# A fixed slot tile per expert in a routed expert layer, with weight blocks of 64 KB in place of 96 KB

## The chip, the cores and the metric

One core of a Trainium2 chip runs the whole program. The metric is the device time of one execution in microseconds, from the first instruction to the last, with what lies around it. The kernel before takes 2897.25 us, the median of 3 runs (2891.38 to 2900.32).

## The reference, cut to what matters

Eight layers act on 4096 tokens of 128 numbers, in float32: cosine attention, routed experts, a gated recurrence (GLRU), routed experts again with the same weights, a state space layer (mamba), and three more. The change touches the two expert layers alone:

```
logits = x @ router_w.T + expert_bias          # 4096 tokens x 160 experts
probs = sigmoid(logits); top_w, top_idx = top_k(probs, 8)
top_w = 2.5 * top_w / (sum(top_w) + 1e-9)
h1 = silu(x @ w_gate[e].T)                     # 64 wide, for each expert e
out[t] = sum over the 8 experts e of t of top_w[t, e] * (h1 @ w_down[e].T) + shared expert
```

So each token meets 8 of 160 experts, and an expert is a gate matrix of 128x64 and a down matrix of 64x128. The tokens reach each layer as a layer norm of the running sum X.

## The kernel before, in words

X stays in SBUF. An expert layer (`run` 0 and 1) is worked in two halves (`h`) of 2048 tokens, 16 tiles of 128 tokens each. It has four parts.

**Routing** (`route_half`, L1634): layer norm, router product on PE, sigmoid on ACT, the eight largest on DVE, and a 0/1 MASK of 128 tokens x 160 experts for each tile.

**Slots** (`slots` L1641, `place` L1667, `rows_of_slots` L1680, on PE `count` L1873 and `rank` L1885): each assignment of a token to an expert gets a row in a DRAM table `slot_rows`. PE counts the tokens of each expert. DVE rounds the counts up to tiles of 128 rows, sums them over the experts, and so finds the first row of each expert and the expert of each tile. Then, tile after tile of tokens, `rank` adds the tokens that stand earlier to psum bank 7, `place` masks it (L1673) and takes the eight row numbers with one MAX8 (L1676), and the next `rank` waits for L1673. After each four tiles `rows_of_slots` works out the 32 row numbers per partition in six small operations (L1683 to L1691). POOL's `dispatch` (L1718) then writes each token's row with 8 indirect DMAs per tile, 128 per half.

**Expert groups** (`experts_scalar` L1767, `experts_sync` L1810, `experts_tensor` L1892, `results_out` L1693): each half has 288 slot tiles, in 72 groups of 4. Per group ACT's queue loads 256 KB of rows into XSB; PE transposes 4 tiles (L1900), ACT copies them (L1779); PE multiplies by the gate matrices (L1909), ACT takes silu (L1786), PE multiplies by the down matrices (L1918), DVE copies the results out of psum (L1699), and ACT's queue stores 256 KB to `slot_results`. SP's queue loads the weights of the 4 tiles: it reads four expert numbers into registers (L1815) and issues four DMAs of 96 KB (L1819). All buffers of a group are four deep (UNROLL), and SP may load the weights of group g only when the results of group g-4 are done (L1829). PE's order in each step is transposes of g+2, gate products of g+1, results of g. PE uses its array in parts: the gate products of two tiles stand in the two column halves (128x64 each), the result products in the two row halves (64x128 each).

**Gather** (`gather` L1728, `sum_rows` L1702): POOL fetches the 8 result rows of each token, DVE adds them weighted to X. Half 0 is gathered while half 1 is computed, half 1 while the next layer runs.

`middle_vector` and its neighbours (L1945 to L2065) write out each engine's order by hand. In run 0 both halves are routed and placed first. In run 1 half 0 is routed between steps 3 and 4 of the GLRU, its later places stand inside GLRU steps 4 to 6 (`between`), and half 1 is routed after the last GLRU step. Each engine is an in-order queue, with semaphores in between. During layer 0 SP's queue also prepares `expert_blocks` (L2098 to L2102) and zeroes `slot_rows`.

## Time and profile before

| | |
|---|---|
| runs, median (lowest, highest) | 2897.25 us (2891.38, 2900.32) |
| the profiled execution's own time | 2902.76 us |
| its span | 2900.9 us |
| mean granted TensorE clock | 0.723 |
| PE busy | 1753.3 us (60%) |
| DVE, ACT, POOL busy | 1334.2, 970.8, 1057.4 us |
| bytes moved by DMA | 393.39 MB |
| packets: under 512 B, under 2 KB, all | 57952, 222512, 332506 |
| waits of PE's gate product (L1909) for the weights | 271.0 us |

The span is that of the one core. A share of busy time is an average over stages with different limits: the four stretches of expert groups make up a third of the span, and there the DMA engines are nearly always busy. DMA issues are not counted as busy time of an engine. In the table of groups, the idle time stands beside what ended it.

### The profile page before, as it was taken

To read this page: it belongs to the slowest core of one execution; us is meant where nothing else is said; L and a number is where in the kernel's file an instruction comes from. 1 tells how busy PE (TensorE), PEld (TensorE's weight loads), DVE (VectorE), ACT (ScalarE), POOL (GpSimd) and SP (SyncE) were. 2 spreads that over 40 slices of the span, in tenths; PEclk is the share of its full clock that TensorE was granted. 3 is DMA by queue.
4 is the path that set the end of the run, shared out by engine and by line. 5 is a ranking of instruction groups with operands and counts; after the bars stand their busy time and mean duration, and the time that the engine had idled before them with its cause. 6 is when DMAs were issued, how large, how long until landed. Compare 5 with 4: busy or idle time off the path is not lost.

```text
span 2900.9 us, 44112 instructions
## 1 busy us (share of the span) xinstructions
PE 1753.3 (60%) x13716; PEld 1146.8 (40%) x13716; DVE 1334.2 (46%) x3558; ACT 970.8 (33%) x1719; POOL 1057.4 (36%) x1177
## 2 busy tenths in 40 slices
PE   3765506776666454556776676422325488888975
PEld 2544404555444242244554454100124234455443
DVE  3648811222334677473222333543215466666644
ACT  3651102232223321312232222356761123444342
POOL 2001777724651774757714651771000200000000
PEclk9985557778878655557788787655555568998985
DMA  8941118999997111117999997120000000000001
GB/s 234 382 181 29 51 53 275 325 304 292 321 289 241 52 52 54 52 55 244 327 308 294 310 301 241 51 54 8 4 2 0 0 1 1 1 1 2 1 1 29
DMA packets 332506, 393.39 MB, mean 136 GB/s; under 512 B 57952, under 2 KB 222512, under 8 KB 332208
## 3 DMA queue, kind: packets, MB, share of 16 engines
q1 hardware_dynamic: 215616, 171.43, 19.0%
q10 hardware_dynamic: 83984, 153.13, 15.4%
q0 software_dynamic: 32768, 67.17, 7.7%
q8 instruction: 65, 1.06, 0.1%
q14 instruction: 73, 0.60, 0.1%
HBM read 242.13 MB, written 164.63 MB: 140 GB/s over the span
## 4 chain that ended last, share of the span: by engine, by line
PE 36%; DVE 15%; DMA 13%; ACT 11%; issue 10%; SPq 9%; POOL 6%; DVEq 0%; ACTq 0%; POOLq 0%
DMA arena<-expert_blocks 12%; SPq L1819 6%; ACT arena L955 5%; PE psum L1918 4%; PE psum L1909 4%; POOL slot_rows L1725 4%; PE psum L448 3%; SPq L1815 3%; PE psum L1347 2%; PE psum L1900 2%; PE psum L1328 2%; PE psum L432 2%; PE psum L993 1%; PE psum L427 1%; ACT arena L1210 1%
## 5 line engine op out<-in xcount | busy, mean ns | idle before, releaser
L1736 POOL DMA_INDIRECT arena<-slot_results,SLOTS x512 | 490.7, 958 | 503.1 <-DMA slot_results<-arena 285.8
L1725 POOL DMA_INDIRECT slot_rows<-arena,SLOTS x512 | 493.4, 964 | 309.4 <-issue 308.8
L1699 DVE COPY arena<-psum 128x512 f32<-128x512 f32 x288 | 198.6, 690 | 742.3 <-PE psum L1918 719.4
L1909 PE MATMUL psum<-arena 128*64 128x128 f32 x2304 | 236.5, 336 | 278.4 <-DMA arena<-expert_blocks 271.0
L1779 ACT ACTIVATE arena<-psum 128x512 f32<-128x512 f32 x288 | 171.9, 597 | 476.4 <-PE psum L1900 467.6
L1909 PEld LDWEIGHTS psum<-arena 128*64 128x64 f32 x2304 | 154.5, 165 | 349.0 <-issue 291.5
L169 POOL TENSOR_SCALAR rstd<-mv 128x4 f32<-128x4 f32 x32 | 6.2, 193 | 772.3 <-DVE mv L577 771.8
L1900 PE MATMUL psum<-ident,arena 128*128 128x128 f32 x1152 | 231.6, 335 | 84.9 <-DMA arena<-slot_rows 84.3
L1918 PE MATMUL psum<-arena 64*128 64x128 f32 x2304 | 253.3, 350 | 0.0
L1786 ACT ACTIVATE arena<-psum 128x256 f32<-128x256 f32 x288 | 110.4, 383 | 338.5 <-PE psum L1909 335.3
L1918 PEld LDWEIGHTS psum<-arena 64*128 64x128 f32 x2304 | 189.6, 230 | 64.4 <-issue 64.2
L1900 PEld LDWEIGHTS psum<-ident,arena 128*128 128x128 f32 x1152 | 149.6, 166 | 130.0 <-issue 93.4
L1710 DVE SCALAR_TENSOR_TENSOR X<-arena,WEIGHTS,X 128x128 f32<-128x128 f32 x512 | 180.2, 352 | 39.9 <-DMA arena<-slot_results,SLOTS 23.9
L955 ACT ACTIVATE arena<-arena 128x1 f32<-128x1 f32 x510 | 150.0, 294 | 16.5
L602 PE MATMUL psum<-ident,XN 128*128 128x128 f32 x192 | 44.4, 376 | 169.4 <-DVE XN L590 165.1
L1101 DVE TENSOR_REDUCE arena<-psum 128x1 f32<-128x128 f32 x256 | 74.0, 289 | 101.4 <-PE psum L1347 96.6
L1210 ACT ACTIVATE arena<-psum 128x1536 f32<-128x1536 f32 x64 | 92.8, 1449 | 80.5 <-PE psum L432 80.5
L602 PEld LDWEIGHTS psum<-ident,XN 128*128 128x128 f32 x192 | 33.2, 197 | 199.7 <-issue 188.2
L1102 DVE TENSOR_REDUCE arena<-psum 128x1 f32<-128x256 f32 x256 | 105.8, 413 | 0.0
L448 PE MATMUL psum<-arena 128*32 128x256 f32 (+1 forms) x1536 | 95.9, 357 | 8.6 <-ACT arena L1210 5.4
L448 PE MATMUL psum<-arena,ones 128*32 128x256 f32 (+1 forms) x1536 | 89.1, 336 | 0.0
L427 PE MATMUL psum<-arena 51*128 51x256 bf16 (+1 forms) x384 | 64.4, 283 | 40.1 <-ACT arena L349 22.5
(234 smaller groups left out, 3064.5 us busy)
## 6 DMA issues: line engine op xcount, KB each, us to landing
arena<-expert_blocks SPq DMA_DIRECT2D x1152, 96.0 KB
arena<-slot_rows ACTq DMA_DIRECT2D x288, 256.0 KB
slot_results<-arena ACTq DMA_DIRECT2D x288, 256.0 KB
slot_rows<-zeros SPq DMA_DIRECT2D x2, 18432.0 KB, 84.2
slot_rows<-arena,SLOTS POOLq DMA_INDIRECT x512, 2.2
arena<-slot_results,SLOTS POOLq DMA_INDIRECT x512
expert_blocks<-in_expert_w SPq DMA_DIRECT2D x1, 7680.0 KB, 26.0
expert_blocks<-in_expert_w SPq DMA_DIRECT2D x1, 5120.0 KB, 52.7
```

Of the source, the lines that this page charges most:

```text
L448: mm = pe.matmul(psum[32 * r:32 * r + 32, 3, 256 * half + lo:256 * half + hi], ones4[:, head_of(n, r) % 4, :] if half else vp(kt, head_of( ...
L955: act.activation(H[:, g, t:t + 1], U[:, g, t:t + 1], ACT.Tanh, bias=H[:, g, t - 1:t]).then_inc(m_h[g], 1)
L1210: act.activation(PR2[:, g % 2], psum[:, 4:8, 0:384], ACT.Exp, scale=DH ** -0.5).then_inc(r_exp.sem, 1)
L1699: dve.tensor_copy(YSB[:, p].rearrange("p (c h) d -> p h c d", h=2), psum[:, first:first + 2, 0:256].rearrange("p h (c d) -> p h c d", c=2) ...
L1710: dve.scalar_tensor_tensor(X[:, t, :], GATHERED[:, j, k], WEIGHTS[:, t, k:k + 1], X[:, t, :], ALU.mult, ALU.add).then_inc(g_sum.sem, 1)
L1725: pool.indirect_dma_start(out=slot_rows[h], out_offset=bass.IndirectOffsetOnAxis(ap=SLOTS[:, t, k:k + 1], axis=0), in_=XNH[:, t], in_offse ...
L1736: pool.indirect_dma_start(out=GATHERED[:, t % TPI, k], out_offset=None, in_=slot_results[h], in_offset=bass.IndirectOffsetOnAxis(ap=SLOTS[ ...
L1779: act.activation(XSBT[:, g % UNROLL], psum[:, g % 2, :], ACT.Copy).then_inc(c_xt.sem, 1)
L1819: sp.dma_start(EWB[:, p, q], expert_blocks[bass.ds(e * P, P), :]).then_inc(c_ew[p].sem, 16)
L1900: mm = pe.transpose(psum[:, p % 2, P * q:P * q + P], XSB[:, p, q], ident[:])
L1909: mm = pe.matmul(psum[lo:lo + INTER, 2 + 5 * (p % 2), o:o + P], EWB[:, p, q, 0:INTER], XSBT[:, p, P * q:P * q + P], start=True, stop=True, ...
L1918: mm = pe.matmul(psum[:, 3 + 2 * (p % 2) + q % 2, c:c + P], HEB[lo:lo + INTER, p % 2, c:c + P], EWB[lo:lo + INTER, p, q, INTER:EW], start= ...
```

## The change: what it does

Each expert now owns one slot tile of 128 rows whatever its count (160 own tiles, 40 groups). An expert with more than 128 tokens in the half takes its further rows from 128 overflow tiles (32 groups), which are handed out as before by counts. There are still 72 groups of 4 tiles; GROUP_ORDER mixes the two kinds evenly.

Because own tiles have known experts, their weights are loaded with fixed addresses: four DMAs, each of 32 partitions with 2 KB in a row. Overflow groups still read four expert numbers and issue four DMAs of 128 pieces of 512 B. For that `expert_blocks` is laid out by partition, and a block is 128x128 (64 KB): 64 columns of gate, 64 of down. The down matrix is cut in column halves, of which one stands in partitions 0 to 63, the other in 64 to 127. So that each result half finds its silu in its own partitions, the gate matrix must stand twice side by side: DVE writes that copy (`gates_twice`), the gate product gives 128 output rows instead of 64, silu covers 512 columns instead of 256, and the results are 8 products of 64x128 by 64x64 per group instead of 4 of 64x128 by 64x128.

Slot numbers need more work: after each four tiles DVE compares, shifts the rows beyond the own tile, scans over 640 elements, masks, takes MAX8, and subtracts neighbours.

```diff
-        EW = INTER + D
+        EW = INTER + D // 2
...
+        GROUP_ORDER = sorted(range(GROUPS), key=lambda n: (n + 0.5) / OWN_GROUPS if n < OWN_GROUPS else (n - OWN_GROUPS + 0.5) / MORE_GROUPS)
...
+        def own_tiles(dve):
+
+            dve.tensor_tensor_scan(OWN_END, ones_row[:], ones_row[:], 0.0, ALU.mult, ALU.add).then_inc(o_own, 1)
...
+            dve.tensor_scalar(OWN_END, OWN_END, float(P), None, ALU.mult).then_inc(o_own, 1)
...
+            dve.tensor_scalar(OWN, OWN_END, -float(P), None, ALU.add).then_inc(o_own, 1)
...
         def slots(dve, run, h):
...
+            dve.tensor_scalar(NTILES, NTILES, 0.0, None, ALU.max).then_inc(link.sem, link.one())
...
+            dve.tensor_tensor(DELTA, DELTA, OWN_END, ALU.subtract).then_inc(link.sem, link.one())
...
         def place(dve, run, t):
...
-            dve.max(S8[:, j], SLOTM[:, j]).then_inc(s_s8.sem, 1)
...
         def rows_of_slots(dve, run, i):
...
-            dve.tensor_scalar(SLOT[:], S8[:], -1.0, None, ALU.add).then_inc(s_slot.sem, 1)
...
+            dve.tensor_tensor(OVER, SLOTM, every(OWN_END), ALU.is_gt).then_inc(link.sem, link.one())
+            dve.wait_ge(link.sem, link.so_far())
+            dve.tensor_tensor(OVER, OVER, every(DELTA), ALU.mult).then_inc(link.sem, link.one())
+            dve.wait_ge(link.sem, link.so_far())
+            dve.tensor_tensor(OVER, SLOTM, OVER, ALU.add).then_inc(link.sem, link.one())
...
+            dve.tensor_tensor_scan(PLACED.rearrange("p t e -> p (t e)"), ones_row[:, 0:1].broadcast_to([P, TPI * NE]), OVER.rearrange("p t e -> p (t e)"),
+                                   0.0, ALU.mult, ALU.add).then_inc(link.sem, link.one())
...
+            dve.tensor_tensor(PLACED, PLACED, MASK[:, TPI * i:TPI * i + TPI, :], ALU.mult).then_inc(link.sem, link.one())
...
+            for j in range(TPI):
+                last = TOPK * (TPI - 1 - j)
+                dve.max(S8[:, last:last + TOPK], PLACED[:, j]).then_inc(link.sem, link.one())
...
+            dve.scalar_tensor_tensor(SLOT[:].rearrange("p t k -> p (t k)"), S8[:, 0:TPI * TOPK], -1.0, S8[:, 1:TPI * TOPK + 1],
+                                     ALU.add, ALU.subtract).then_inc(link.sem, link.one())
...
+        def gates_twice(dve, run, h, g):
+
+            p, hr = g % UNROLL, HALVES * run + h
+            dve.wait_ge(c_ew[p].sem, c_ew[p].at(hr, g // UNROLL))
+            dve.tensor_copy(GATES[:, p], EWB[:, p, :, 0:INTER].unsqueeze(2).broadcast_to([P, GROUP, 2, INTER])).then_inc(c_twice.sem, 1)
...
             def gated(g):
-                act.activation(HEB[:, g % 2], psum[:, 2 + 5 * (g % 2), 0:256], ACT.Silu).then_inc(c_he.sem, 1)
+                act.activation(HEB[:, g % 2], psum[:, 2 + 5 * (g % 2), :], ACT.Silu).then_inc(c_he.sem, 1)
...
         def experts_sync(sp, run, h):
...
+            def own_weights(n, p):
+                for part in range(GROUP):
+                    rows = slice(P // GROUP * part, P // GROUP * (part + 1))
+                    sp.dma_start(EWB[rows, p].rearrange("p q c -> p (q c)"), expert_blocks[rows, GROUP * EW * n:GROUP * EW * (n + 1)]).then_inc(c_ew[p].sem, 16)
...
-                    sp.dma_start(EWB[:, p, q], expert_blocks[bass.ds(e * P, P), :]).then_inc(c_ew[p].sem, 16)
+                    sp.dma_start(EWB[:, p, q], expert_blocks[:, bass.ds(e * EW, EW)]).then_inc(c_ew[p].sem, 16)
...
             def inner(g, p):
-                pe.wait_ge(c_ew[p].sem, c_ew[p].at(hr, g))
+                pe.wait_ge(c_twice.sem, c_twice.at(hr, g, p + 1))
...
-                    mm = pe.matmul(psum[lo:lo + INTER, 2 + 5 * (p % 2), o:o + P], EWB[:, p, q, 0:INTER], XSBT[:, p, P * q:P * q + P],
-                                   start=True, stop=True, skip_group_check=True, tile_position=(0, lo))
+                    mm = pe.matmul(psum[:, 2 + 5 * (p % 2), P * q:P * q + P], GATES[:, p, q].rearrange("p a c -> p (a c)"),
+                                   XSBT[:, p, P * q:P * q + P], start=True, stop=True, skip_group_check=True)
...
             def results(g, p):
...
-                    mm = pe.matmul(psum[:, 3 + 2 * (p % 2) + q % 2, c:c + P], HEB[lo:lo + INTER, p % 2, c:c + P],
-                                   EWB[lo:lo + INTER, p, q, INTER:EW], start=True, stop=True, skip_group_check=True, tile_position=(lo, 0))
+                    for half in range(2):
+                        lo = INTER * half
+                        mm = pe.matmul(psum[:, 3 + 2 * (p % 2) + half, INTER * q:INTER * q + D // 2], HEB[lo:lo + INTER, p % 2, P * q:P * q + P],
+                                       EWB[lo:lo + INTER, p, q, INTER:], start=True, stop=True, skip_group_check=True, tile_position=(lo, 0))
...
         def middle_vector(dve):
...
                 for g in range(GROUPS):
+                    if g + 2 < GROUPS:
+                        gates_twice(dve, run, 0, g + 2)
                     results_out(dve, run, 0, g)
...
-            whole = a["expert_w"].rearrange("(e p) c -> e p c", p=P)
-            block_of = expert_blocks.rearrange("(e p) c -> e p c", p=P)
+            whole = a["expert_w"].rearrange("(e p) c -> p e c", p=P)
+            block_of = expert_blocks.rearrange("p (e c) -> p e c", c=EW)
```

## Rows read from the trace of the kernel before

**Rows 1.** Stretches: us; PE, PEld, DVE, ACT, POOL busy; PEclk, DMA share, GB/s.

```profile
447.00:684.00 237.00, 170.81 (x1440) 125.26 (x1440) 49.67 (x72) 71.56 (x145) 119.70 (x125) 0.80 0.95 309
684.00:933.00 249.00, 167.94 (x1440) 123.04 (x1440) 93.98 (x208) 72.04 (x146) 121.16 (x128) 0.80 0.93 297
...
sum 970.00, PE 673.61 PEld 493.66 DVE 287.02 ACT 285.95 POOL 475.47; mean PE 168.40 PEld 123.41 DVE 71.76 ACT 71.49 POOL 118.87
```

**Rows 2.** DMA queues (packets, MB, share), 447 to 684: ACT's, SP's, POOL's.

```profile
q10 hardware_dynamic: 20457, 37.26, 46.2%
q1 hardware_dynamic: 40307, 27.53, 39.2%
q0 software_dynamic: 4064, 8.33, 9.2%
```

**Rows 3.** Chain of waits, 611 to 625 us: start, duration, what.

```profile
611.50 0.02 SPq L161
...
614.02 4.92 DMA arena<-expert_blocks
...
624.74 0.02 SPq L161
```

**Rows 4.** Timeline of PE, expert groups: start, duration, line, shapes.

```profile
619.16 1.12 PE L1909 MATMUL psum<-arena 128*64 128x128 f32 x8 [2.78 <-DMA arena<-expert_blocks]
...
622.41 1.12 PE L1909 MATMUL psum<-arena 128*64 128x128 f32 x8
...
625.55 0.66 PE L1909 MATMUL psum<-arena 128*64 128x128 f32 x8
626.14 0.72 PE L1918 MATMUL psum<-arena 64*128 64x128 f32 x8
626.79 0.66 PE L1900 MATMUL psum<-ident,arena 128*128 128x128 f32 x4
627.37 0.66 PE L1909 MATMUL psum<-arena 128*64 128x128 f32 x8
```

**Rows 5.** Timeline of PE elsewhere, eight fp32 passes on the whole array.

```profile
1092.74 1.13 PE L1856 MATMUL psum<-w_sh_gate,arena 128*128 128x64 f32 x8
2847.43 1.16 PE L822 MATMUL psum<-w_wv_t,arena 128*128 128x128 f32 x8 [0.66 <-DVE arena L752]
```

**Rows 6.** Timeline, last place of the first four tiles, and what follows.

```profile
277.57 0.32 DVE L1673 SCALAR_TENSOR_TENSOR arena<-psum,arena 128x160 f32<-128x160 f32 x1
279.54 0.32 DVE L1673 SCALAR_TENSOR_TENSOR arena<-psum,arena 128x160 f32<-128x160 f32 x1
280.46 1.22 POOL L1725 DMA_INDIRECT slot_rows<-arena,SLOTS  x1 [106.01 <-issue]
```

**Rows 7.** Groups by line: busy us, mean ns of one, idle before.

```profile
L1620 DVE TENSOR_TENSOR arena<-arena 128x640 f32<-128x640 f32 x16 | 13.2, 825 | 0.5
L1618 DVE TENSOR_TENSOR_SCAN arena<-ones_row,arena 128x160 f32<-128x160 f32 x64 | 26.3, 473 | 2.3
L653 DVE TENSOR_TENSOR_SCAN arena<-arena 128x256 f32<-128x256 f32 x16 | 10.2, 678 | 1.4 <-DVE arena L647 1.4
L1624 DVE MAX8 C<-arena 128x8 f32<-128x160 f32 x64 | 16.2, 315 | 2.4
```

**Rows 8.** Timeline of DVE, a place inside the GLRU and DVE's next work.

```profile
1145.11 0.33 DVE L1673 SCALAR_TENSOR_TENSOR arena<-psum,arena 128x160 f32<-128x160 f32 x1
1148.82 0.69 DVE L661 TENSOR_TENSOR arena<-psum,arena 128x512 f32<-128x512 f32 x1 [1.84 <-ACT arena L689]
```

**Rows 9.** Timeline, the last place of run 1 and PE's first gate product.

```profile
1318.89 0.33 DVE L1673 SCALAR_TENSOR_TENSOR arena<-psum,arena 128x160 f32<-128x160 f32 x1
1321.30 1.12 PE L1909 MATMUL psum<-arena 128*64 128x128 f32 x8
```

**Rows 10.** Two further stretches in the columns of Rows 1.

```profile
180.00:200.00 20.00, 17.58 (x295) 11.49 (x296) 5.44 (x9) 10.74 (x10) 0.00 (x0) 0.96 0.01 3
380.00:447.00 67.00, 0.00 (x0) 0.00 (x0) 0.00 (x0) 0.00 (x0) 50.75 (x53) 0.50 0.16 56
```

More of the change, by code:

```diff
@@ L1646, in slots @@
             dve.wait_ge(link.sem, link.so_far())
-            dve.tensor_scalar(COUNT, COUNT, P - 1, None, ALU.add).then_inc(link.sem, link.one())
+            dve.tensor_scalar(COUNT, COUNT, -1, None, ALU.add).then_inc(link.sem, link.one())
             dve.wait_ge(link.sem, link.so_far())
@@ L1673, in place @@
             dve.scalar_tensor_tensor(SLOTM[:, j], psum[:, 7, 0:NE], 1.0, MASK[:, t, :], ALU.add, ALU.mult).then_inc(s_slotm.sem, 1)
-            dve.wait_ge(s_slotm.sem, s_slotm.at(run, t))
-            stand(dve)
-            dve.max(S8[:, j], SLOTM[:, j]).then_inc(s_s8.sem, 1)
             if j == TPI - 1:
@@ L1687, in rows_of_slots @@
[L1687 to L1691 removed]
+            link = Order(s_slot, run, i)
@@ new lines, in rows_of_slots @@
+            every = lambda row: row.unsqueeze(1).broadcast_to([P, TPI, NE])
+            dve.wait_ge(s_slotm.sem, s_slotm.at(run, TPI * i + TPI - 1))
+            dve.tensor_tensor(OVER, SLOTM, every(OWN_END), ALU.is_gt).then_inc(link.sem, link.one())
+            dve.wait_ge(link.sem, link.so_far())
+            dve.tensor_tensor(OVER, OVER, every(DELTA), ALU.mult).then_inc(link.sem, link.one())
+            dve.wait_ge(link.sem, link.so_far())
+            dve.tensor_tensor(OVER, SLOTM, OVER, ALU.add).then_inc(link.sem, link.one())
@@ L1878, in count @@
             mm.then_inc(e_cnt.sem, 1)
-            pe.wait_ge(o_link.sem, o_link.at(run, h))
-            pe.matmul(psum[:, 7, 0:NE], ident[:], FIRST, start=True, stop=True, skip_group_check=True)
+            pe.wait_ge(o_own, 3)
+            pe.matmul(psum[:, 7, 0:NE], ident[:], OWN, start=True, stop=True, skip_group_check=True)
+            pe.wait_ge(o_col.sem, o_col.at(run, h))
             for q in range(GROUP):
@@ L1947, in middle_vector @@
             dve.memset(C9[:], 0.0)
+            dve.memset(S8[:], 0.0)
+            own_tiles(dve)
             for h in range(HALVES):
@@ L1953, in middle_vector @@
             for run in range(HALVES):
+                for g in range(2):
+                    gates_twice(dve, run, 0, g)
                 for g in range(GROUPS):
+                    if g + 2 < GROUPS:
+                        gates_twice(dve, run, 0, g + 2)
                     results_out(dve, run, 0, g)
+                for g in range(2):
+                    gates_twice(dve, run, 1, g)
                 for g in range(GROUPS):
+                    if g + 2 < GROUPS:
+                        gates_twice(dve, run, 1, g + 2)
                     results_out(dve, run, 1, g)
@@ L2097, in _ @@
             sp.wait_ge(loaded, 16 * (FIRST_WEIGHTS + 1))
-            whole = a["expert_w"].rearrange("(e p) c -> e p c", p=P)
-            block_of = expert_blocks.rearrange("(e p) c -> e p c", p=P)
-            sp.dma_start(block_of[:, 0:INTER], whole[:, 0:INTER]).then_inc(blocked, 16)
-            sp.dma_start(block_of[:, INTER:, 0:INTER], whole[:, INTER:, 0:INTER]).then_inc(blocked, 16)
-            sp.dma_start(block_of[:, INTER:, INTER:], whole[:, 0:INTER, INTER:]).then_inc(blocked, 16)
+            whole = a["expert_w"].rearrange("(e p) c -> p e c", p=P)
+            block_of = expert_blocks.rearrange("p (e c) -> p e c", c=EW)
+            sp.dma_start(block_of[:, :, 0:INTER], whole[:, :, 0:INTER]).then_inc(blocked, 16)
+            for half in range(2):
+                sp.dma_start(block_of[INTER * half:INTER * half + INTER, :, INTER:], whole[0:INTER, :, INTER + D // 2 * half:INTER + D // 2 * (half + 1)]).then_inc(blocked, 16)
             sp.wait_ge(constants, 14)
```

97 lines of the change are left out of this document (57 added, 40 removed).

## The prediction

> **What bounds the kernel now.** I read the stretches first. Four of them hold the expert groups, 72 groups each: half 0 takes 237 us, half 1 takes 249 us, and with their like in run 1 they make 970 us [rows 1]. That is 3.29 and 3.46 us per group. In them the DMA engines show a share of 0.95 and 0.93, PE is busy for 171 of 237 us at a granted clock of 0.80, and DVE, ACT and POOL have much room [rows 1]. Next the queues: in half 0, ACT's queue (rows in, results out) takes 46.2% of the engines' time, SP's (weights) 39.2%, POOL's (scatter) 9.2% [rows 2]. Last the chain of waits, for what a full DMA does to the order of work: it goes round a ring of four groups. SP is released at 611.50, its fourth issue is out at 614.02, the weights land 4.92 us later, PE works 5.6 us, and SP is released again at 624.74 [rows 3]. That is 13.24 us for four groups, or 3.31 per group, which is the stretch's pace. So weights bound these stretches, by bytes and by latency at once; PE idles about 66 us per half.
>
> Ahead of the groups lie chains that the change lengthens: DVE's slot numbers, which release POOL's dispatch in run 0, and DVE and PE in turn in run 1.
>
> **DMA work of a group.** A weight packet now costs 0.392 x 16 x 237 us / 36,864 = 40 ns (768 B; the 3,443 others are small and counted in). ACT's 18,432 packets of 2 KB cost 95 ns each by the same division [rows 2]. A line through both gives 7.5 ns + 0.0427 ns per byte, so 29 ns for 512 B, an estimate from these rows. The 40 own groups need 128 packets of 2 KB, the 32 overflow groups 512 of 512 B: (5,120 x 95 + 16,384 x 29) / 16 = 60 us of all engines per half, against 93 now. With ACT's 109.5 and POOL's 21.8 unchanged, half 0 needs 192 us of DMA instead of 224. At today's 0.95 that is 202 us; half 1, by the same saving, 215. If bytes count and not packets (73.2 MB less 9.4), the bounds are 206 and 217. Above that the only bound is no gain at all, 237, should 512 B pieces at a wide pitch cost the 40 ns of 768 B and more.
>
> **PE work of a group.** At the full clock today: gate products 0.59 us (625.55 to 626.14), results 0.65, transposes 0.58, together 1.82 us; at the half clock the same three take 3.25 us (619.16 to 622.41) [rows 4]. After:
> - Gate products: 8 passes on the whole array in place of 8 on halves. Such passes take (1.16 - 0.27) / 7 = 0.127 us each at the full clock, with 0.27 us the last one's tail [rows 5]. 8 x 0.127 = 1.02 us.
> - Results: 16 passes with 64 moving columns in place of 8 with 128. No row shows that form packed in row halves. Below: the moving columns are the same in number, so 0.65 us. Above: the unpacked form with 64 columns costs (1.13 - 0.27) / 7 = 0.122 us [rows 5], 16 x 0.122 = 1.95 us. I take 0.078 us per pass. Two packed passes today cost 2 x 0.081 = 0.162 us, 0.035 more than one unpacked pass of the same width (0.127); I put the same 0.035 on the unpacked narrow pass, (0.122 + 0.035) / 2. That gives 1.25 us.
> - Transposes stay at 0.58.
>
> Sum 2.85 us, or 205 us per half at the full clock (2.25 to 3.55 us, 162 to 256 us, by the two bounds). At the half clock, in proportion, 3.25 x 2.85 / 1.82 = 5.1 us. So PE, today with a third of its time idle, comes level with DMA.
>
> The first row on this is that 8 result passes with 128-column weights take 0.65 us, 81 ns each, at the full clock [rows 4]. The Trainium skill (TensorE: Matmul & The Clock Gate, "LDWEIGHTS (loading the stationary operand)") says that a weight load costs its columns divided by 1.2, whatever the rows: 107 ns here. By that rule 16 result passes could not be under 1.71 us, the group would be 3.3 us and half 0 would gain nothing. The 81 ns contradict the rule as a floor for packed loads, so the sum stays with the rows.
>
> **The ring after.** From one release of SP to the next, at the full clock: issue 2.1 us (2.5 today [rows 3]; the register load goes in 40 of 72 groups), flight 3.9 us (4.92 today; a quarter of the packets in the own groups, bounds 2.5 and 5.5), DVE's copy of the gates 0.8 with a wait behind L1699 (640 elements take 0.825 [rows 7], 512 so 0.66), PE 1.02 + 1.25 + 2.85 = 5.1. Sum 11.9 us, 2.98 per group. Three limits so stand close together (DMA 2.8, PE 2.85, ring 2.98), and where one is late the others can't make it up. I add 2% for that and take 3.05 in half 0 if the clock were full, and 3.1 in half 1, where the DMA has 8 us more to do. The clock: PE falls to half speed after waits such as the 2.78 us before 619.16 and is back by 625.55 [rows 4]. With PE over 90% busy such waits must be rare; I take 3% of the groups at 5.1. The result is 3.11 and 3.16 us per group, 224 and 228 us. Against 237 and 249, twice, the stretches give back 2 x (13 + 21) = 68 us.
>
> The rest of the edit inside the groups is hidden. Silu over 512 columns: ACT is busy 72 of 237 us [rows 1] and works a step ahead of PE. The gate copies add 72 x 0.66 = 48 us to DVE's 94 in half 1 [rows 1]; DVE copies two groups ahead, so the 3 us of a gather sum in front of one copy fits in two groups of PE work. If that cover failed, each of 16 sums per half would cost up to 3 us, 96 us in all.
>
> **Slot numbers.** For four tiles, the last place and the first of the next four lie 1.97 us apart, with 0.32 for L1673 itself [rows 6]. Of the work in between, 0.4 us (one MAX8) goes, and there come: compare, multiply, add and mask, four operations over 640 elements, 4 x 0.87 with the step between them [rows 7]; one scan over 640, (0.678 - 0.473) / 96 per element, 1.5 us (up to 4 x 0.473 = 1.9) [rows 7]; four MAX8 in a row, 4 x 0.25 = 1.0 (0.315 each, overlapped [rows 7]); a small subtraction for a small one. In all 3.5 + 1.5 + 1.0 + 0.2 - 0.4 = 5.8 us more. Where this is late:
> - Run 0, half 0, first four tiles: POOL starts at 280.46 [rows 6] and issues on, one DMA in 1.26 us, until the groups start (53 in the last 67 us, with every other engine idle [rows 10]), so all of it counts: 5.8. `own_tiles` adds 1.3 at the start of routing, `slots` 0.3 for one operation on 160 elements, and the first rank matrix no longer waits for DVE, -0.9. Sum 6.5. The other seven blocks of run 0 delay only DVE's routing, which is done 67 us ahead of POOL [rows 10]: 7 x 5.8 = 41 us fit in, nothing.
> - Run 1, half 0, first four: the GLRU's front stands behind it in DVE's queue: 5.8 - 0.6 = 5.2.
> - Three blocks inside the GLRU: after the place at 1145.11 DVE's next work starts at 1148.82 [rows 8]. The chain now ends at 1145.44 + 7.4 = 1152.8, so 4.0 us each, 12.0.
> - Run 1, half 1: nothing stands between the places and the groups. Three blocks of 5.8, less 0.6: 16.8. The fourth holds back the first gate copy: today the first gate product starts 2.1 us after the last place ends [rows 9], then 7.4 + 0.7 = 8.1 us after, so 6.0.
>
> Sum 6.5 + 5.2 + 12.0 + 22.8 = 46.5 us. Bounds 35 (small operations overlap more) and 60.
>
> **The preparation of the blocks** becomes 40,960 pieces of 256 B. DMA is idle from 180 us on [rows 10] and the first scatter is at 280 us, so up to 100 us more are hidden; past that each microsecond delays POOL.
>
> **Sum.** 2902.8 (the profiled execution) - 68 + 46.5 = 2881; that execution is 5.5 us above the median, so 2876 us.
>
> **Rivals.**
> A. PE becomes the bound and slower than today's pace. Place: the results products; price: 0.107 to 0.122 us per pass instead of 0.078, 3.3 to 3.55 us per group. It decides from 0.107 on: half 0 no longer gains. For it: the form is unknown, and the narrow unpacked pass is hardly cheaper than the wide one [rows 5]. Against: halves do overlap today. At 0.122, 256 us in each of four stretches, +54 and +46: 2997; at 0.107, 240 each, -10 and +46: 2933.
> B. The clock stays at 0.80 as today, 40% of the groups' time at the half clock: 0.6/3.05 + 0.4/5.1 = 0.275 groups per us, 3.63 us, 262 us per stretch: 3016. For it: PE's waits for weights are what drops the clock, and some will remain. Against: a PE that is always due has no waits of 2.8 us.
> C. The narrow passes cost near their floor (0.06 us) and DMA alone sets the pace: 202 and 215 us, -136 and +46: 2807. For it: packing hid half the time so far. Against: the ring needs 2.9.
> D. The change doesn't do what it says: 512 B pieces cost as much as 768 B, and the ring stays at 3.2 to 3.3: -25 and +46: 2918.
>
> **How the numbers follow.** Forecast 0.40 (its own range 2850 to 2906), C 0.18, D 0.16, A 0.17, B 0.09. A measurement here tells about 0.3%, 8.7 us, from no change: faster is below 2888.6, same up to 2905.9. The forecast's mass is three quarters faster, the rest nearly all the same; C is faster; D is a quarter same, the rest slower; A and B slower. Faster 0.48, same 0.14, slower 0.38. The range leaves out the lower end of C and A's upper half with B: 2810 to 2965.
>
> **What would show it.** Right: weight packets fall to 60 us of engine time per half; L1900's group period near 3.1; PE busy over 90% of a stretch at a clock over 0.9; results pass 0.078 at the full clock; POOL's first scatter about 6.5 us later; the stretch from GLRU's fourth step to the groups about 40 us longer. Wrong: PE idle as before, a clock near 0.8, or result passes over 0.1.

## The result, and the profile after

The changed kernel takes 2968.61 us, the median of 4 runs (2959.92 to 2976.76), against 2894.32 us for the kernel before in its 4 runs beside it (2889.72 to 2900.32). The ratio is 1.0255, 95% interval [1.0219, 1.0291]: 74 us slower. I had forecast 2876 us. The profiled execution after took 2959.92 us with a span of 2958.0 us, 57.1 us more than the span before.

Where the 57.1 us stand, from the first and last work of the expert groups in the two traces:

| stretch | before | after | change | forecast |
|---|---|---|---|---|
| start to the first group of run 0 | 447.42 | 465.49 | +18.1 | +6.5 |
| the two halves of run 0 | 483.0 | 482.0 | -1.0 | -34 |
| to the first group of run 1 | 389.0 | 421.4 | +32.4 | +34.0 |
| the two halves of run 1 | 481.1 | 486.4 | +5.3 | -34 + 6.0 |
| to the end | 1100.4 | 1102.7 | +2.3 | 0 |

The 68 us that the stretches were to give back did not come at all. Of the 79 us between the forecast for the profiled execution (2881) and its time (2960), 66 lie in the stretches. The other 12 lie outside them, nearly all in the first row. Here are the four stretches of the changed kernel ("after" from here on), in the columns of [rows 1]: time; PE, PEld, DVE, ACT, POOL busy; granted clock, DMA share, GB/s.

```profile
465.00:702.00 237.00, 208.42 (x2016) 185.92 (x2016) 76.79 (x144) 87.29 (x145) 121.48 (x125) 0.90 0.85 274
702.00:948.00 246.00, 210.82 (x2016) 187.76 (x2016) 118.20 (x269) 86.00 (x144) 122.14 (x128) 0.90 0.83 258
1369.00:1607.00 238.00, 202.98 (x2016) 182.12 (x2016) 85.04 (x162) 87.28 (x145) 110.19 (x112) 0.92 0.83 266
1607.00:1855.00 248.00, 215.72 (x2014) 193.75 (x2016) 119.06 (x268) 85.89 (x144) 122.58 (x128) 0.87 0.83 255
sum 969.00, PE 837.93 PEld 749.56 DVE 399.08 ACT 346.45 POOL 476.40; mean PE 209.48 PEld 187.39 DVE 99.77 ACT 86.61 POOL 119.10
```

The DMA engines did get their relief (share 0.95 to 0.85, rate 309 to 274 GB/s), and the clock rose (0.80 to 0.90). The time is what it was. PE is busy 208 of 237 us and the DMA share is 0.85: neither is full. The queues of half 0, as in [rows 2]:

```profile
q10 hardware_dynamic: 20687, 37.66, 46.1%
q1 hardware_dynamic: 25807, 18.75, 29.2%
q0 software_dynamic: 4064, 8.33, 9.6%
```

Weights take 0.292 x 237 = 69 us of all engines, where [rows 2] gave 93 and I had worked out 60. The chain of waits, in the part that answers to [rows 3]:

```profile
568.65 0.02 SPq L161
...
568.73 0.45 SPq L1872
...
571.28 3.81 DMA arena<-expert_blocks
...
575.12 0.44 DVE arena L1738
...
575.60 1.16 PE psum L1964 x8
576.75 1.06 PE psum L1974 x16
...
577.83 0.02 SPq L161
```

Read it from one release of SP (568.65) to the next (577.83): 2.6 us for the register load and four issues, 3.8 in flight, 0.44 for the gate copy, then the gate products of that group, and behind them, in the same step, the results of the group before. That last operation is what SP waits for. So one turn of 9.2 us covers three groups and not four: 3.06 us per group in this turn, in which nothing waits for a busy engine. Over the whole half, from the end of the fourth group's results to that of the last, the trace gives 3.16 us per group. The rest of the 237 us is the start of the stretch: 17.7 us pass from the first transposes to the end of the fourth results. In the kernel before it was 16.7 us, and then 3.19 per group. Next PE's timeline at the full clock, and one operation of each kind at the half clock (start, duration, line, shapes, wait):

```profile
577.72 0.66 PE L1956 MATMUL psum<-ident,arena 128*128 128x128 f32 x4
578.27 1.16 PE L1964 MATMUL psum<-arena 128*128 128x128 f32 x8
579.36 1.11 PE L1974 MATMUL psum<-arena 64*128 64x64 f32 x16
580.40 0.66 PE L1956 MATMUL psum<-ident,arena 128*128 128x128 f32 x4
583.94 1.15 PE L1964 MATMUL psum<-arena 128*128 128x128 f32 x8 [0.33 <-DVE arena L1738]
...
486.52 1.97 PE L1974 MATMUL psum<-arena 64*128 64x64 f32 x16
...
601.57 1.91 PE L1964 MATMUL psum<-arena 128*128 128x128 f32 x8
```

From start to start, gate products take 1.09 us (1.02 forecast), the 16 result passes 1.04 us, 0.065 each (1.25 and 0.078 forecast), transposes about 0.55. A group costs PE 2.7 us, less than my 2.85. Yet it waits again and again for L1738, the gate copy, and so in the end for weights:

```profile
L1964 PE MATMUL psum<-arena 128*128 128x128 f32 x2304 | 356.8, 304 | 119.2 <-DVE arena L1738 118.7
L1974 PE MATMUL psum<-arena 64*128 64x64 f32 x4608 | 344.8, 293 | 0.0
L1738 DVE COPY arena<-arena 128x512 f32<-128x512 f32 x288 | 126.7, 441 | 345.1 <-DMA arena<-expert_blocks 344.1
```

Those are groups of the page (busy us, mean ns, idle before). DVE's copies themselves wait 344 us for the weights. PE's wait in front of the gate products fell from 271 us to 119, while its work in the stretches grew by 164 us (673.61 in [rows 1] to 837.93): the waits were filled with work, and nothing was left over.

### The profile page after: what moved, and what is told of

Read it like the earlier page. It is cut to its first block, busy times and chain, and to the rows that moved or that the text cites. A ratio compares the mean times of both kernels' runs of the same rounds, so it can differ in the third digit from the quotient of the medians.

```text
span 2958.0 us, 46720 instructions
## 1 busy us (share of the span) xinstructions
PE 1922.6 (65%) x16020; PEld 1404.0 (47%) x16020; DVE 1517.2 (51%) x3938; ACT 1032.8 (35%) x1719; POOL 1082.8 (37%) x1177
## 4 chain that ended last, share of the span: by engine, by line
PE 40%; DVE 19%; ACT 11%; DMA 10%; issue 9%; POOL 6%; SPq 5%; DVEq 0%; ACTq 0%; POOLq 0%
DMA arena<-expert_blocks 9%; PE psum L1964 6%; PE psum L1974 6%; ACT arena L955 5%; POOL slot_rows L1776 4%; PE psum L448 3%; SPq L1876 2%; DVE X L1757 2%; PE psum L1956 2%; PE psum L1347 2%; PE psum L1328 2%; PE psum L432 2%; PE psum L993 1%; PE psum L427 1%; ACT arena L1210 1%
## 5 line engine op out<-in xcount | busy, mean ns | idle before, releaser
L1776 POOL DMA_INDIRECT slot_rows<-arena,SLOTS x512 | 515.0, 1006 | 331.8 <-issue 331.8
L1964 PE MATMUL psum<-arena 128*128 128x128 f32 x2304 | 356.8, 304 | 119.2 <-DVE arena L1738 118.7
L1964 PEld LDWEIGHTS psum<-arena 128*128 128x128 f32 x2304 | 317.3, 213 | 148.4 <-DVE arena L1738 120.4
L1974 PE MATMUL psum<-arena 64*128 64x64 f32 x4608 | 344.8, 293 | 0.0
L1830 ACT ACTIVATE arena<-psum 128x512 f32<-128x512 f32 x288 | 172.0, 597 | 488.1 <-PE psum L1956 487.1
L1974 PEld LDWEIGHTS psum<-arena 64*128 64x128 f32 x4608 | 304.1, 202 | 38.2 <-issue 8.8
L1738 DVE COPY arena<-arena 128x512 f32<-128x512 f32 x288 | 126.7, 441 | 345.1 <-DMA arena<-expert_blocks 344.1
L1837 ACT ACTIVATE arena<-psum 128x512 f32<-128x512 f32 x288 | 172.0, 597 | 277.1 <-PE psum L1964 275.6
L1956 PE MATMUL psum<-ident,arena 128*128 128x128 f32 x1152 | 205.8, 306 | 60.5 <-DMA arena<-slot_rows 60.0
L1956 PEld LDWEIGHTS psum<-ident,arena 128*128 128x128 f32 x1152 | 133.2, 151 | 82.0 <-issue 50.2
```

The costliest lines, as they stand in the source:

```text
L1738: dve.tensor_copy(GATES[:, p], EWB[:, p, :, 0:INTER].unsqueeze(2).broadcast_to([P, GROUP, 2, INTER])).then_inc(c_twice.sem, 1)
L1776: pool.indirect_dma_start(out=slot_rows[h], out_offset=bass.IndirectOffsetOnAxis(ap=slots_of(t, k), axis=0), in_=XNH[:, t], in_offset=None ...
L1830: act.activation(XSBT[:, g % UNROLL], psum[:, g % 2, :], ACT.Copy).then_inc(c_xt.sem, 1)
L1837: act.activation(HEB[:, g % 2], psum[:, 2 + 5 * (g % 2), :], ACT.Silu).then_inc(c_he.sem, 1)
L1956: mm = pe.transpose(psum[:, p % 2, P * q:P * q + P], XSB[:, p, q], ident[:])
L1964: mm = pe.matmul(psum[:, 2 + 5 * (p % 2), P * q:P * q + P], GATES[:, p, q].rearrange("p a c -> p (a c)"), XSBT[:, p, P * q:P * q + P], sta ...
```

## Experiments

The stretches of each are read from its own trace with the same cut (first transposes to last results); before gives 964 us and after 968 in that cut. A trace shows one execution, which can lie off its kernel's median, and where that matters it is said. The kernel before was run beside the others each time: it took 2901 us beside the first four, and 2889 beside the next four.

**The two parts alone.** The slots without the blocks:

```diff
-        EW = INTER + D // 2
+        EW = INTER + D
```

and with it the 96 KB blocks, packed products and 256-column silu of before.

> Fixed slot tiles, overflow tiles and the mixed order of groups, with the blocks, products and silu of the kernel before (own tiles load their 96 KB blocks from fixed addresses). Theory 1, the slot numbers: the DVE chain of 7.3 us per four tiles, and POOL held up by DVE's long operations, cost all of what lies outside the group stretches, +50 to +55 us; the stretches stay at 237 and 249 us, since their DMA work is unchanged: 2940 to 2955 us. Rival, the mixed order or the fixed loads matter: fixed loads spare SP 0.5 us per own group, which shortens the ring, 5 to 8 us per stretch less, 2915 to 2930 us.

Measured 2910.91 us, ratio 1.0042 [1.0020, 1.0064]. The blocks without the slots (EW as in the change, the doubled gates, 16 narrow result passes, every expert number read at run time):

> The 64 KB blocks, the doubled gate matrix and the narrow result products, with the slots of the kernel before, so that every group reads its experts at run time and loads 512 pieces of 512 B. Theory 1: the price of the whole change lies in the slot numbers, and what the blocks save in DMA is lost again to the longer ring (DVE's copy, longer products) and PE's half clock: stretches within 5 us of 237 and 249, in all 2885 to 2910 us. Rival, the blocks save 16 us or more per stretch by themselves (DMA work 192 in place of 224 us): 2830 to 2850 us. Second rival, PE's added work costs more than the DMA saves: 2920 us or more.

Measured 2958.79 us, ratio 1.0177 [1.0152, 1.0202]. The first stretch of each, slots alone and then blocks alone:

```profile
463.00:696.00 233.00, 164.90 (x1441) 120.93 (x1441) 49.70 (x72) 71.76 (x145) 119.61 (x126) 0.81 0.96 317
```

```profile
450.00:707.00 257.00, 220.03 (x2017) 198.04 (x2018) 77.63 (x144) 87.09 (x145) 121.58 (x126) 0.85 0.80 253
```

All four stretches take 922 us with the slots alone (-42) and 1036 with the blocks alone (+71). The profiled execution of the blocks alone was the slowest of its five, 21 us above their median, so about +50 is nearer to a usual one. So the slots save in the stretches and the blocks cost there, though the blocks are the part that takes load off DMA (0.95 to 0.80). The slots alone still lose slightly, since what they add outside the stretches, 45 us, is more than the 42. Neither is what I expected. The slots were to leave the stretches as they were, and the rival, 5 to 8 us less in each, went the right way but not far enough. The blocks did worse than my 2885 to 2910, as their second rival said. The slots come with two things, fixed expert numbers and the mixed order of groups; no run parts them.

**The rings deeper.** All rings of a group in SBUF (rows, weights, gate copies, results) six steps deep, in after and in before. For the two further steps, semaphores serve that the first layer no longer needs.

```diff
-        UNROLL = 4
+        UNROLL = 6
```

> The changed kernel with all rings of the groups six deep in place of four, nothing else. Theory 1, the ring: weights are released by the results of four groups before, but PE does the gate products of one group ahead of the results, so only three groups cover issue (2.6 us), flight (3.8 to 5), DVE's copy (0.5) and two products (2.2); with six, five groups cover them and the limit moves to DMA (share 0.85 of 237 us, so 201 us of work) or PE (2.52 us per group at the full clock, 181 us): 205 to 215 and 213 to 225 us per stretch, 2865 to 2885 us in all. Rival, DMA packets or PE's clock set the pace and depth changes nothing: 2955 to 2970 us.

Measured 2781.81 us, ratio 0.9581 [0.9558, 0.9605], 83 us below the lower end of what I expected.

> The kernel before with all rings of the groups six deep. Theory 1, there DMA is full (share 0.95 and 0.93), so depth can win only what is missing to 1: 3 to 6 us per stretch of half 0 and 8 to 12 of half 1, 2865 to 2880 us. Rival, also there the ring's latency sets the pace and the share shown is inflated by queueing: 15 us or more per stretch, under 2840 us.

Measured 2799.57 us, ratio 0.9642 [0.9621, 0.9664], where the rival had it. The first two stretches of after with six deep and, below them, the first of before with six deep:

```profile
460.00:652.00 192.00, 184.52 (x2016) 170.25 (x2016) 75.71 (x144) 87.19 (x145) 120.83 (x125) 0.98 0.99 339
652.00:857.00 205.00, 187.70 (x2016) 170.06 (x2016) 116.20 (x269) 86.02 (x144) 122.95 (x128) 0.99 0.96 307
```

```profile
448.00:667.00 219.00, 156.57 (x1440) 115.29 (x1440) 49.70 (x72) 71.72 (x145) 120.04 (x125) 0.85 1.00 334
```

This one edit is worth 171 us of stretches in after (968 to 797) and 107 in before (964 to 857). Not an instruction or a byte of a group is saved by it. PE is now busy 184.5 of 192 us, and its timeline goes round with almost no wait: PE's own passes bound this stretch now. (In the second half of each run the same kernel needs 2.79 us per group; why stays open.) Here one step, from gate products (L1972 there) over results (L1982) to the next gate products:

```profile
580.39 1.06 PE L1972 MATMUL psum<-arena 128*128 128x128 f32 x8
581.38 1.11 PE L1982 MATMUL psum<-arena 64*128 64x64 f32 x16
...
582.91 1.06 PE L1972 MATMUL psum<-arena 128*128 128x128 f32 x8
```

2.52 us per group. The clock follows: of the 144 groups of run 0, the transposes ran at the half clock in 50 in before, in 19 in after, and in 6 in after with six deep, which are the first three groups of each half (1.1 us in place of 0.66 for four tiles). With the waits gone the low clock is gone, so it was mostly a result of them. And the share of 0.95 that I had taken as DMA at its bound was none: with six deep before moved 334 GB/s where it had moved 309.

What depth bought can be read from SP. Its waits for results in the first stretch of before and, below it, of before with six deep (waited for, us, times, longest):

```profile
SPq L161 <- PE psum L1918: 184.1, 22, 166.7
```

```profile
SPq L161 <- PE psum L1926: 162.5, 1, 162.5
```

The longest wait is the one for the half's first results. Without it, SP stood waiting for 17.4 us of the stretch in before, and not at all with six deep. In after it was 58.5 us, and 5.9 with six deep. So the turn through the buffers held SP back far more in after than in before. In before SP's own stream of register loads and issues was nearly as long as the turn.

**Taking PE's and DVE's share out of the turn.** Two kernels on the changed one. In the first there is no gate copy: the gate product waits for the weights themselves and multiplies by a buffer of zeros, so the output of the experts is left out, while every operation on PE stays.

```diff
-                pe.wait_ge(c_twice.sem, c_twice.at(hr, g, p + 1))
+                pe.wait_ge(c_ew[p].sem, c_ew[p].at(hr, g))
```

> The changed kernel without the copy that doubles the gates: the gate product waits for the weights themselves and reads a GATES tile set once to zero. It leaves out the gate matrices. All products, silus and DMAs stay. Theory 1: the ring becomes 0.5 us shorter per three groups, in half 1 more, where the copy also waits behind gather sums: 0.17 us and more per group, 12 to 20 us per stretch, 2890 to 2920 us. Rival, the copy is hidden: 2955 us or more.

Measured 2932.02 us, ratio 1.0146 [1.0095, 1.0196]: less was gained than I expected, though more than the rival allows. The second also goes back to the packed products of before, on the 64 KB blocks: 8 gate passes on column halves and 8 result passes of 64 moving columns, so half of the result products is left out.

> The changed kernel with its slots, blocks and DMAs, but with the products of the kernel before: gate products of two tiles in the two column halves, 8 result passes per group over 128 columns of the block, silu over 256, no doubling copy on DVE. It leaves out the right result: the result products read gate columns as if they were the down matrix's. Theory 1, the ring of three covering groups: issue 2.6, flight 4, products 1.2 instead of 2.1 and no copy of 0.5, so 7.8 us per three groups in place of 9.2: DMA then binds, 207 to 215 us per stretch, 2840 to 2870 us. Rival, SP's issue or DMA's small pieces alone set the pace: 2940 us or more.

Measured 2852.16 us, ratio 0.9876 [0.9819, 0.9933]. First stretches, without the copy and then with the packed products:

```profile
464.00:698.00 234.00, 205.90 (x2017) 185.46 (x2018) 49.76 (x72) 87.25 (x145) 119.68 (x125) 0.91 0.87 278
```

```profile
465.00:682.00 217.00, 161.38 (x1440) 118.79 (x1439) 49.69 (x72) 71.82 (x145) 119.44 (x125) 0.83 0.93 299
```

The four stretches take 932 and 848 us, against 968 (the profiled execution is the fastest of its kernel in all three). A copy of 0.44 us on an engine that is busy 77 of 237 us costs 0.13 us per group on average. That is near the 0.15 that a turn for three groups would give (0.44 / 3), but it is no proof of the third: the first stretch gained 3 us and the others 9 to 13. And 45 us less PE work per half (205.90 to 161.38) give back 21 us per half, though PE was not full before. PE at its bound would not have answered to the copy, and DMA at its bound would have answered to neither; a turn of latencies answers to both.

**SP's issues.** The weights of an own group in one DMA of 256 KB in place of four.

```diff
-                for part in range(GROUP):
-                    rows = slice(P // GROUP * part, P // GROUP * (part + 1))
...
+                sp.dma_start(EWB[:, p].rearrange("p q c -> p (q c)"), expert_blocks[:, GROUP * EW * n:GROUP * EW * (n + 1)])
```

> The changed kernel with the weights of an own group in one DMA of 128 partitions x 2 KB instead of four of 32. Theory 1: SP issues an own group in 0.5 us instead of 1.9, so its ring is 1.4 us shorter in 40 of 72 groups, 0.25 us per group on average if all counts: up to 18 us per stretch, half of that where PE or an overflow group binds next: 2900 to 2935 us. Rival, SP's issue is hidden behind the flight of earlier pieces: 2955 us or more.

Measured 2978.22 us, ratio 1.0307 [1.0245, 1.0369], no better than the change itself; the stretches take 984 us. There are three issues fewer, but the one transfer is longer in flight than the last of four. Two such in the chain of waits:

```profile
567.02 4.42 DMA arena<-expert_blocks
...
574.27 5.98 DMA arena<-expert_blocks
```

In the mean over the first stretch it is 4.57 us, against 4.07 for the last quarter of an own group in after. From the first issue to the landing, though, the single transfer is the faster (4.57 against 5.44), and still no time was gained. The table shows where it went: the mean turn of the first stretch, in us, from the results that SP waits for to the results three groups later.

| kernel | wait for SP's queue | first to last issue | flight of the last | copy and its wait | wait for PE | gate product to results | sum |
|---|---|---|---|---|---|---|---|
| before | 1.67 | 1.59 | 4.22 | none | 0.65 | 1.64 | 9.76 |
| after | 0.56 | 1.48 | 3.89 | 0.53 | 0.72 | 2.31 | 9.49 |
| without the copy | 0.58 | 1.50 | 3.93 | none | 1.17 | 2.33 | 9.50 |
| packed products, no copy | 0.70 | 1.54 | 4.25 | none | 0.77 | 1.55 | 8.81 |
| one DMA for own weights | 0.53 | 0.71 | 4.31 | 0.81 | 1.23 | 2.34 | 9.92 |

The sum is three times the pace by its making, so it proves nothing by itself; its parts do. With one DMA the 0.77 us that the issues save came back in front of DVE and PE (0.28 and 0.51) and in the flights (0.42), which made the turn longer than in after. Why PE was later there stays open. Without the copy, too, the wait for PE took most of the 0.53 back in this stretch. So the turn is what paces after, but it has about 1.3 us of queueing in it (0.56 and 0.72), and a piece that is shortened is not always won.

**The slot numbers later.** Six deep, and in run 1 the chains of L1700 moved: those of half 0 by one GLRU step, those of half 1 between the first results of half 0.

```diff
+                    if run and g % 8 == 1 and g // 8 < HSTEPS:
+                        rows_of_slots(dve, 1, HSTEPS + g // 8)
```

> Rings six deep as in after_u6, and in run 1 the slot numbers out of the way: SLOTM holds 16 tiles, the chains of half 1 stand in DVE's queue after results 1, 9, 17 and 25 of half 0's groups, those in the GLRU at the start of the next step, where DVE is idle for 6 us. Theory 1: of the 53 us of slot numbers, 17 + 6 us before the groups of run 1 go, and 3 x 3 us in the GLRU; up to 7 us come back as stalls among the groups: 2745 to 2765 us. Rival, POOL's dispatch of half 1 starts too late or is held up by DVE's chains and the second half waits for it: 2775 us or more.

Measured 2791.58 us, ratio 0.9651 [0.9607, 0.9695], slightly worse than six deep alone. The groups of run 1 do start at 1252.3 us instead of 1275.0, but its first stretch gives it back:

```profile
1252.00:1481.00 229.00, 202.04 (x2016) 186.19 (x2016) 102.11 (x208) 87.28 (x145) 126.59 (x128) 0.88 0.85 279
```

229 us for 197. Of PE's waits in that stretch (engine, line, waited for, us, times, longest) the longest name the gate copies (L1748 in this kernel), which stand behind a chain in DVE's queue:

```profile
PE psum L1974 <- DVE arena L1748: 21.1, 4, 5.3
```

**The slots with six deep**, once more without the blocks.

> Slots of after, with the 96 KB blocks, packed products and loads of before, rings six deep. Theory (with six deep the stretches move bytes at the DMA engines' limit, and the fixed expert numbers only shortened the ring): the stretches stay at the 858 us of before with six deep, the slot numbers add their 50 us: 2840 to 2860 us, ratio 0.98 to 0.99. Rival (the fixed loads save time of their own, as the 42 us at four deep): stretches about 816 us, 2800 to 2815 us, ratio 0.966 to 0.972.

> As the kernel just before, with the slot numbers of run 1 worked out later: those of half 0 one GLRU step on, those of half 1 between the first results of half 0. Theory (in the version with 64 KB blocks the late chains held the gate copies of half 0 up, which took back the 23 us that the groups started earlier; here there are no gate copies): 20 to 30 us less than the kernel just before. Rival (it is the copies of the results out of psum that are held up, and those are here too): the first stretch of run 1 is 20 to 30 us longer, the time within 8 us of the kernel just before.

> The changed kernel; in run 0, from the second block of four tiles on, the compare over 640 elements is done four times and the scan over 640 three times (same result), which gives DVE 3 x 0.87 + 2 x 1.5 = 5.6 us more per block, 39 us in seven blocks, about as much as the change itself gave it there. Theory (POOL's issues of indirect DMAs are held up beside DVE's long operations): POOL's dispatch of run 0 takes 7 to 12 us longer than the 176.9 us of the changed kernel, its mean issue rises from 1.006 to 1.04 to 1.06 us, and the groups start at about 474 us instead of 465.5. Rival (the 10 us came from something else, as more scattered rows or the queue): groups start at 465 to 467.

For these three the kernel before itself took 3621.93 us beside them, on another chip. The ratios to it are 0.9526 [0.9501, 0.9551], 0.9514 [0.9489, 0.9540] and 1.0198 [1.0151, 1.0245], the last from two executions. Their stretches can't be set beside the others, because PE, ACT and DVE stood almost still there for 20 to 30 us at a time while POOL issued its indirect DMAs, as the chain of waits of the first shows:

```profile
596.99 21.99 another core or an unknown queue
619.39 33.19 another core or an unknown queue
```

Why that chip did so I can't tell. The late slots gained nothing there either, but on this ground I leave that comparison open. So the first was run again:

> The same kernel as slots_u6, again, because there the kernel before itself took 3622 us and its stretches can't be set beside those of the other runs. Theory (with six deep the stretches are bound by the DMA engines' work): stretches about 858 us, 2840 to 2860 us, ratio 0.98 to 0.99. Rival (the fixed loads shorten the stretches by some 40 us here too): 2800 to 2815 us, ratio 0.966 to 0.972.

Measured 2790.30 us (before 2896.00), ratio 0.9630 [0.9617, 0.9643], below what even the rival expected; its stretches sum to 803 us, 54 less than before with six deep.

```profile
465.00:667.00 202.00, 156.67 (x1440) 115.35 (x1440) 49.70 (x72) 71.77 (x145) 119.29 (x125) 0.83 1.04 363
```

The same bytes per group at 363 GB/s in place of 334. In before with six deep the chain of waits runs through SP's queue, where register loads and issues follow on each other without a wait:

```profile
573.92 0.73 SPq L1823
574.81 0.33 SPq L1827
...
577.25 0.89 SPq L1823
```

From one register load to the next (L1823) 3.3 us pass, with four issues (L1827) between; the stretch's mean is 219 / 72 = 3.04 us per group. With no wait for results in the whole stretch (above), it is SP's own work that sets the pace there, and fixed numbers take the load away in 40 of 72 groups. That this, and not the mixed order, is what the slots save fits with SP's waits: they come back with the slots (14 us in the first stretch). The best kernel is the change with six deep, 2782 us; slots alone or before with six deep come within 0.6% of it by their ratios to before.

## Why the prediction was wrong

**The step that failed** is the sum that follows "The ring after", from which the 3.11 and 3.16 us per group came. Three things in it were wrong.

First the count. I counted 2.1 us of issue, 3.9 in flight, 0.8 of copy and 5.1 of PE and divided by four groups. The turn holds only 2.2 us of PE, and it serves three groups, because PE does the results of the group before right behind the gate products, and SP waits for those. The turn that I had read [rows 3] misled me: PE had fallen behind and did two steps in it at the half clock, so it served four groups in 13.24 us. That my 2.98 us came near the 3.06 of the measured turn is luck: too much work was divided by too many groups, and my own pieces counted rightly give 9.07 / 3 = 3.02.

Second, a term at nothing. The start of a stretch was not in the sum. In half 0 it adds 9 us to 72 groups at 3.16, which is 0.13 us per group. I had missed it because the one turn that I read, 3.31, happened to equal the mean of the stretch before, 3.29, whose own steady pace was 3.19. So of the 0.18 us per group by which half 0 missed, the ring is 0.08 and the start 0.13; my allowance for clock and disturbance (0.13) was even 0.03 too large. In half 1 the steady pace was 3.34 against my 3.16. Part of that is the gate copies, which stand behind the gather sums in DVE's queue: without them it is 3.26.

Third, what bounded the kernel before. I held DMA to be full, and gave SP's own stream no limit. Its stretch speeds up with deeper rings by 21 us, so DMA was not full, and SP waited for results in only 17 us of it.

**The two effects that cancelled.** Flight shortened (4.22 to 3.89 us in the mean), and the slots helped (-42 us, slots alone). But the copy (0.44 us), wider gate products and the narrow results (together 0.98 us more in the turn) were added where the latency lies. I had counted them in the ring, but in a ring of four, and let PE's waits vanish. Six deep showed that the same work can run at 2.52 us per group once the latency is covered.

**The clock.** I allowed 3% of the groups at the half clock. In run 0 it was 13% (19 of 144), as waits remained. The six-deep kernel shows 4% (6 of 144), so the 3% would have been nearly right had the waits gone.

**DMA work.** 201 us per half by the shares after (0.461 + 0.292 + 0.096 of 237) against 192 forecast. In the trace of after a packet of 512 B takes 29.0 ns in the mean, as forecast. Of the 9 us that the weights took beyond my 60, 7 lie in their packets of 2 KB (116 ns each, where I had 95) and the rest in packets of 4 bytes that I had not counted. It did not matter: DMA was not the bound.

**PE work.** Results at 0.065 us per pass were below my 0.078; rival A, which needed 0.107, did not come to pass, though its time (2933 to 2997) holds the result. The Trainium skill (TensorE: Matmul & The Clock Gate, "LDWEIGHTS (loading the stationary operand)") would have 107 ns for each weight load of 128 columns. These passes of 65 ns contradict it as a floor for loads into row halves, as the 81 ns of before did.

**Slot numbers.** The places stand as forecast. At the first four tiles, then inside the GLRU, then at the end of run 1 (timeline of after: start, duration, line):

```profile
280.00 0.33 DVE L1696 SCALAR_TENSOR_TENSOR arena<-psum,arena 128x160 f32<-128x160 f32 x1 [0.54 <-PE psum L1946]
287.72 0.33 DVE L1696 SCALAR_TENSOR_TENSOR arena<-psum,arena 128x160 f32<-128x160 f32 x1
288.64 1.22 POOL L1776 DMA_INDIRECT slot_rows<-arena,SLOTS  x1 [111.84 <-issue]
...
1233.18 0.33 DVE L1696 SCALAR_TENSOR_TENSOR arena<-psum,arena 128x160 f32<-128x160 f32 x1 [0.54 <-PE psum L1946]
...
1240.76 0.68 DVE L661 TENSOR_TENSOR arena<-psum,arena 128x512 f32<-128x512 f32 x1
...
1368.38 0.32 DVE L1696 SCALAR_TENSOR_TENSOR arena<-psum,arena 128x160 f32<-128x160 f32 x1 [0.54 <-PE psum L1946]
...
1376.49 2.07 PE L1964 MATMUL psum<-arena 128*128 128x128 f32 x8 [5.63 <-DVE arena L1738]
```

7.72 us for 1.97 [rows 6] is +5.75 (5.8 forecast); 7.58 for 3.71 [rows 8] is +3.9 (4.0); 8.11 us for 2.41 [rows 9] is +5.7 (6.0). The miss is in the first row of the table, +18.1 for +6.5. The start of POOL came 8.2 us later, not 6.5, as layer 0 ran 2 us longer in that execution. And POOL's own 128 issues of half 0 took 172.4 us instead of 162.6 (from the first start to the last end, in the timeline). "The other seven blocks of run 0 delay only DVE's routing: nothing" was wrong for a reason I had not looked for: the issues themselves take longer when one of DVE's long operations is already running.

```profile
311.32 0.96 POOL L1776 DMA_INDIRECT slot_rows<-arena,SLOTS  x1 [0.31 <-issue]
312.59 1.29 POOL L1776 DMA_INDIRECT slot_rows<-arena,SLOTS  x1 [0.30 <-issue]
314.18 2.12 POOL L1776 DMA_INDIRECT slot_rows<-arena,SLOTS  x1 [0.30 <-issue]
...
311.35 0.83 DVE L1705 TENSOR_TENSOR arena<-arena 128x640 f32<-128x640 f32 x1
312.21 0.82 DVE L1707 TENSOR_TENSOR arena<-arena 128x640 f32<-128x640 f32 x1
...
314.04 1.49 DVE L1712 TENSOR_TENSOR_SCAN arena<-ones_row,arena 128x640 f32<-128x640 f32 x1
```

Of the 128 issues 20 took over 1.1 us (4 in before); what all took above 0.958 us sums to 11.1 us (1.3 in before). The lines show when. The first issue starts 0.03 us before the compare of L1705 and takes 0.96. The second starts when L1707 has 0.44 us to go and takes 0.33 longer; the third starts when the scan has 1.35 to go and takes 1.17 longer. The Trainium skill (SBUF — State Buffer, "🔬 SBUF: two separate sides") says that a DVE operation with two SBUF inputs and a GpSimd operation that reads SBUF lock each other out for a whole instruction, whichever starts first. These issues agree: each is longer by the rest of the DVE operation that it found running, less 0.1 to 0.2 us.

The kernel with the compare and the scan repeated was to settle it. Both its expectations failed: POOL took 169.6 us there (my theory said 7 to 12 us more than in after), and the groups started at 553 us, on the chip where all kernels were slower. The mechanism shows in it all the same. Five issues that found a repeated compare running took 1.28 to 1.42 us, and six that found a repeated scan running took about 1.22. In all 21 took over 1.1, yet they summed to only 8.3 us above 0.958, because DVE stood still for over 20 us at a time from 378 us on, while POOL went on. So what costs is an issue that finds such an operation running, and not the sum of DVE's work.

**The rivals.** None of them was what happened. D came nearest in the pace, for the wrong reason: the ring stayed near 3.3 us, though the pieces of 512 B did get cheaper. B's clock of 0.80 did not stay. What I lacked was the rival "the turn of the ring takes all the new work in", with the test that goes with it: does the stretch change when the ring is deeper? (Rival B's sum gives about 3020, not 3016, which changes nothing.)

## What to carry to other kernels

A chain of waits that closes on itself is a bound of its own: count what stands in one turn, and count how many steps it serves from the place of the releasing operation in the engine's order, not from the number of buffers. Two engines at 85 to 95% busy or transferring may both be waiting for the same turn. The queue that issues the transfers is an engine too: count its own loads and issues per step. Add the start of a stretch to its steady pace. Before bytes are traded for work, make the ring deeper, for that costs two buffers and here was worth 3.6% to 6.6%, where the trade itself lost 2.5%. While such a turn sets the pace, added work between a transfer's landing and the release of its buffer is not hidden by its engine's idle time; with a deeper ring it was.

## What the runs showed of the hardware that I had not expected

- A DMA share of 0.95 at 309 GB/s was not the limit: the same core moved 339 (change) and 363 GB/s (slots alone) with six deep, at shares up to 1.05, so that share is no scale that ends at 1.
- With hardly a wait left PE kept a granted clock of 0.98 to 0.99 over 200 us stretches.
- Sixteen passes of 64x128 weights by 64 moving columns in alternating row halves take 0.065 us each in float32, eight with 128 moving columns 0.081.
- An indirect DMA issue of POOL takes 0.96 us, also when a compare over 640 elements starts 0.03 us after it, and up to 2.13 us when it finds a scan of 640 elements running on DVE.
- One load of 256 KB was in flight for 4.57 us in the mean of a stretch (2.6 to 6.9). The same load in four quarters took 5.44 us from the first issue to the last landing, of which 4.07 for the last quarter.
